# Block rows loaded in 256-byte pieces from ScalarE's queue and transposed by VectorE, in a routed feed-forward kernel

## What is computed

```
x = x + attention(layernorm(x), ctx)          # 16 heads of 16
x = x + ffn(layernorm(x))
ffn: logits = xf @ Wr + br;  top 2 of 8 experts, softmax over the two
     h = xf @ W1[e] + b1[e]                   # 256 -> 1024, halves a and g
     out_e = (silu(a) * g) @ W2[e] + b2[e]    # 512 -> 256
     out = sum over the two chosen experts of gate * out_e
```

## Time and profile before

| | |
|---|---|
| median of three runs | 1309.9 us |
| profiled execution, its own time | 1309.45 us |
| its span | 1307.6 us |
| mean granted TensorE clock | 0.959 of full |
| PE, DVE, ACT, POOL busy, share of the span | 91%, 77%, 57%, 48% |

### The profile page before, as it was taken

The page is one execution under the profiler, slowest core; times in us unless marked ns, Lnnn a source line. Parts: engine busy times, 40 slices in busy tenths (PEclk is TensorE's granted clock), DMA queues, the critical chain, the costliest instruction groups (busy, mean ns, idle before and its releaser), DMA issues.

```text
span 1307.6 us, 38188 instructions
## 1 busy us (share of the span) xinstructions
PE 1189.3 (91%) x12680; PEld 1047.7 (80%) x12681; DVE 1001.4 (77%) x2933; ACT 750.2 (57%) x1497; POOL 625.2 (48%) x729
## 2 busy tenths in 40 slices
PE   5999999999999999730699999999999999999986
PEld 4677777777777777520599999999999999999986
DVE  5788888888888878735487888888788888877764
ACT  5676666666666665412456555555655556565452
POOL 5346666666666665542043444444344443432334
PEclk9999999999999999755699999999999999999998
DMA  5123332333333322217667676676767776676553
GB/s 172 35 87 93 98 96 93 100 98 98 101 98 102 94 69 74 76 61 234 192 172 176 170 186 161 182 165 178 179 164 188 162 182 167 175 181 155 147 149 37
DMA packets 106958, 174.78 MB, mean 134 GB/s; under 512 B 13600, under 2 KB 82400, under 8 KB 106848
## 3 DMA queue, kind: packets, MB, share of 16 engines
q1 hardware_dynamic: 77808, 134.45, 32.1%
q0 software_dynamic: 26592, 36.46, 16.7%
q10 hardware_dynamic: 2448, 2.44, 0.6%
HBM read 125.17 MB, written 47.60 MB: 132 GB/s over the span
## 4 chain that ended last, share of the span: by engine, by line
PE 41%; DMA 8%; issue 2%; POOL 1%; SPq 1%; DVE 0%; ACTq 0%; ACT 0%; POOLq 0%; DVEq 0%
PE bank L1071 9%; PE bank L1072 8%; PE bank L1073 8%; DMA out_rows<-y_gated,block_tokens 6%; PE bank L1086 4%; PE bank L1087 4%; PE bank L1088 4%; PE bank L1060 2%; DMA w_raw<-in_L_ffn_W 1%; PE bank L1089 1%; POOL out_rows L1319 1%; SPq L1020 0%; DMA routed_rows<-block_rows 0%; DVE act L1274 0%; ACTq L994 0%
## 5 line engine op out<-in xcount | busy, mean ns | idle before, releaser
L1319 POOL DMA_INDIRECT out_rows<-y_gated,block_tokens x142 | 267.2, 1882 | 435.0 <-DVE y_gated L1289 339.0
L1071 PE MATMUL bank<-block_T_hi,w_hi 128*128 128x256 f32 x1136 | 330.8, 291 | 10.1 <-DVE block_T_lo L1264 10.1
L1073 PE MATMUL bank<-block_T_hi,w_lo 128*128 128x256 f32 x1136 | 319.0, 281 | 0.0
L1072 PE MATMUL bank<-block_T_lo,w_hi 128*128 128x256 f32 x1136 | 319.0, 281 | 0.0
L1071 PEld LDWEIGHTS bank<-block_T_hi,w_hi 128*128 128x128 f32 x1136 | 216.2, 190 | 11.8 <-DVE block_T_lo L1264 8.0
L1072 PEld LDWEIGHTS bank<-block_T_lo,w_hi 128*128 128x128 f32 x1136 | 216.0, 190 | 0.0
L1073 PEld LDWEIGHTS bank<-block_T_hi,w_lo 128*128 128x128 f32 x1136 | 215.3, 190 | 0.0
L1157 ACT ACTIVATE act_hi<-act 128x512 fp32r<-128x512 f32 x142 | 89.8, 632 | 195.3 <-DVE act L1274 195.3
L491 ACT ACTIVATE probs_T<-bank 128x512 f32<-128x512 f32 x256 | 132.2, 603 | 98.3 <-PE bank L322 98.3
L1247 DVE TENSOR_TENSOR w_lo<-w_raw,w_hi 128x1024 fp32r<-128x1024 f32 x142 | 167.7, 1222 | 11.3 <-ACT w_hi L1134 10.9
L599 DVE TENSOR_REDUCE row_max<-bank 128x4 f32<-128x512 f32 x256 | 158.9, 683 | 22.3 <-PE bank L303 22.3
(11 more groups left out here) (159 smaller groups left out, 2494.6 us busy)
## 6 DMA issues: line engine op xcount, KB each, us to landing
w_raw<-in_L_ffn_W SPq DMA_DIRECT2D x71, 1024.0 KB
block_rows<-routed_rows SPq DMA_DIRECT2D x71, 272.0 KB
x_in<-in_x SPq DMA_DIRECT2D x64, 128.0 KB, 2.5
ctx_T<-in_ctx SPq DMA_DIRECT2D x16, 512.0 KB, 4.2
x_res<-in_x SPq DMA_DIRECT2D x64, 128.0 KB, 2.5
out_rows<-x SPq DMA_DIRECT2D x64, 128.0 KB, 2.3
w_raw<-in_L_ffn_W SPq DMA_DIRECT2D x8, 512.0 KB, 7.9
out_rows<-y_gated,block_tokens POOLq DMA_INDIRECT x142, 4.3
```

Source lines behind the costliest of these rows:

```text
L1071: mm(dst, w1h[:, k, c, at:at + P], xh[:, k, c, :], start=(c == 0), stop=False)
L1072: mm(dst, w1h[:, k, c, at:at + P], xl[:, k, c, :], start=False, stop=False)
L1073: last = mm(dst, w1l[:, k, c, at:at + P], xh[:, k, c, :], start=False, stop=(c == KC - 1))
L1319: nc.gpsimd.indirect_dma_start(out=out[:, :], out_offset=bass.IndirectOffsetOnAxis(ap=tk[:, u % U, t:t + 1], axis=0), in_=yg[:, u % 2, t, ...
```

## The change

Only `experts` changes.

- SP no longer loads block rows. Its slot holds `load_w1` alone, which is now two DMAs of 512 KB instead of one of 1 MB; the rows of W1 go to other partitions, matching the new order of the features.
- ScalarE's queue loads block rows, at the end of its slot, for block b+3. There are five DMAs for a block: four that fill 32 partitions each with pieces of 256 bytes (1024 pieces in all), and one for the last 16 floats of each row (256 pieces of 64 bytes) into a buffer of its own, `block_marks`. The two waits of `load_rows` come along. At the start the first two loads stand ahead of `w1_hi(0, 0)`, and the third behind `x_hi(0, 0)`.
- The four transposes on PE are gone. VectorE transposes all 32x32 squares of 128x512 in one instruction (`square`), between `w1_lo` and `mult` of the first half, from SBUF to SBUF.
- `x_hi` and `x_lo` read SBUF instead of PSUM. The moving operand of the 48 up matmuls is read in eight runs of 32 elements instead of one of 256. The idle rows have a buffer of their own.

```diff
-        xb = sb("block_rows", [P, 2, ET, ROW], F32)
+        xb = sb("block_rows", [P, 2, NJ, KC, DT], F32)
+        xm = sb("block_marks", [P, 2, ET, ROW - D], F32)
+        xT = sb("block_T", [P, NJ, KC, DT], F32)
+        pad_t = sb("idle_rows", [P, ET, ROW], F32)
...
         @block.sync
-            def load_rows(i, u):
...
-                sp.dma_start(w1r[:, u % 2], ... "(c p) n -> p c n" ...).then_inc(s_w1[u % 2], 16)
+                w = w1....rearrange("(p c i) n -> c p i n", c=KC, i=DT)
+                for c in range(KC):
+                    sp.dma_start(w1r[:, u % 2, c, :], w[c]).then_inc(s_w1[u % 2], 16)
...
             def slot(i, u):
                 if real(i, u + 2):
-                    load_rows(i, u + 2)
                     load_w1(i, u + 2)
...
         @block.tensor
-            def to_T(i, u):   # four transposes, L1053 to L1062
...
-                        mm(dst, w1h[:, k, c, at:at + P], xh[:, k, c, :], start=(c == 0), stop=False)
+                        mm(dst, w1h[:, k, c, at:at + P], xh[:, k, :, c, :], start=(c == 0), stop=False)
...
         @block.scalar
+                act.wait_ge(s_pd, 16 * (E + 2))
+                load_rows(0, 0)
+                load_rows(0, 1)
                 w1_hi(0, 0)
                 x_hi(0, 0)
+                load_rows(0, 2)
+
+            def load_rows(i, u):
+
+                r = act.value_load(tab[0:1, 1, bass.ds(blk(i, u), 1)], min_val=0, max_val=E * REG)
+                if real(i, u - 2):
+                    act.wait_ge(s_xT, n(i, u - 2))
+                    act.wait_ge(s_meta, n(i, u - 2))
+                rows = xs[bass.ds(r, EB), :]
+                for p in range(NP):
+                    act.dma_start(xb[p * DT:(p + 1) * DT, u % 2].rearrange("k j c i -> k j (c i)"),
+                                  rows[:, p * KC * DT:(p + 1) * KC * DT].rearrange("(j k) m -> k j m", k=DT)
+                                  ).then_inc(s_ld[u % 2], 16)
+                act.dma_start(xm[:, u % 2], rows[:, D:ROW].rearrange("(t p) c -> p t c", p=P)).then_inc(s_ld[u % 2], 16)
...
                 act_hi(i, u, 1)
+                if real(i, u + 3):
+                    load_rows(i, u + 3)
...
         @block.vector
+            def square(i, u):
+
+                dve.wait_ge(s_ld[u % 2], n2(i, u, NP + 1))
+                if real(i, u - 1):
+                    dve.wait_ge(s_xl, n(i, u - 1))
+                V.transpose(xT[:].rearrange("p j c k -> p (j c k)"),
+                            xb[:, u % 2].rearrange("p j c i -> p (j c i)")).then_inc(s_xT, 1)
...
             def slot(i, u):
                 if real(i, u + 1):
                     w1_lo(i, u + 1)
+                    square(i, u + 1)
                 mult(i, u, 0)
```

More of the change, by code:

```diff
@@ L912, in experts @@
     HM = FC // 2
+    NJ = EB // DT
+    NP = P // DT
     with ExitStack() as ctx:
@@ L938, in experts @@
         prf = sb("idle_at_f", [1, E], F32)
-        xb = sb("block_rows", [P, 2, ET, ROW], F32)
+        xb = sb("block_rows", [P, 2, NJ, KC, DT], F32)
+        xm = sb("block_marks", [P, 2, ET, ROW - D], F32)
+        xT = sb("block_T", [P, NJ, KC, DT], F32)
+        pad_t = sb("idle_rows", [P, ET, ROW], F32)
         tk = sb("block_tokens", [P, U, ET], I32)
         gt = sb("block_gates", [P, U, ET], F32)
-        pad = xb[:, 1]
-        xh = sb("block_T_hi", [P, 2, KC, EB], F32R)
-        xl = sb("block_T_lo", [P, 2, KC, EB], F32R)
+        pad = pad_t[:]
+        xh = sb("block_T_hi", [P, 2, NJ, KC, DT], F32R)
+        xl = sb("block_T_lo", [P, 2, NJ, KC, DT], F32R)
         sa = sb("silu_a", [P, FC, EB], F32)
@@ L985, in n, with n2 @@
             return i * (U * per) + (u * per + (per if done is None else done))
-        def n2(i, u):
-            return i * (U // 2 * 16) + (u // 2 + 1) * 16
+        def n2(i, u, parts):
+            return i * (U // 2 * 16 * parts) + (u // 2 + 1) * 16 * parts
         def idle_rows(eng, experts):
@@ L1012, in load_w1 @@
                     sp.wait_ge(s_w1l, n(i, u - 2, KC))
-                sp.dma_start(w1r[:, u % 2], w1.rearrange("e k n -> (e k) n")[bass.ds(e * D, D), :]
-                             .rearrange("(c p) n -> p c n", p=P)).then_inc(s_w1[u % 2], 16)
+                w = w1.rearrange("e k n -> (e k) n")[bass.ds(e * D, D), :].rearrange("(p c i) n -> c p i n", c=KC, i=DT)
+                for c in range(KC):
+                    sp.dma_start(w1r[:, u % 2, c, :], w[c]).then_inc(s_w1[u % 2], 16)
             def first():
@@ L1025, in first @@
                 load_w1(0, 0)
-                sp.wait_ge(s_pd, 16 * (E + 2))
-                load_rows(0, 0)
-                load_rows(0, 1)
                 load_w1(0, 1)
@@ L1050, in first @@
                 nc.tensor.transpose(bank[5][:, 0:E * 2 * FC], b1r[:], ident[0:E * 2 * FC, 0:E * 2 * FC]).then_inc(s_b1t, 1)
-                to_T(0, 0)
-            def to_T(i, u):
[L1055 to L1062, removed]
             def up(i, u, bk, half, side):
@@ L1068, in up @@
                     at = side * F + (HM * half + m) * P
-                    dst = bk[:, m * EB:(m + 1) * EB]
+                    dst = bk[:, m * EB:(m + 1) * EB].rearrange("p (j k) -> p j k", k=DT)
                     for c in range(KC):
-                        mm(dst, w1h[:, k, c, at:at + P], xh[:, k, c, :], start=(c == 0), stop=False)
-                        mm(dst, w1h[:, k, c, at:at + P], xl[:, k, c, :], start=False, stop=False)
-                        last = mm(dst, w1l[:, k, c, at:at + P], xh[:, k, c, :], start=False, stop=(c == KC - 1))
+                        mm(dst, w1h[:, k, c, at:at + P], xh[:, k, :, c, :], start=(c == 0), stop=False)
+                        mm(dst, w1h[:, k, c, at:at + P], xl[:, k, :, c, :], start=False, stop=False)
+                        last = mm(dst, w1l[:, k, c, at:at + P], xh[:, k, :, c, :], start=False, stop=(c == KC - 1))
                 return last
@@ L1103, in slot @@
                     up(i, u, bank[2 * half + 1], half, 1).then_inc(s_g, 1)
-                    if half == 0 and real(i, u + 1):
-                        to_T(i, u + 1)
                 if real(i, u - 1):
@@ L1125, in first @@
                 act.dma_start(xs[E * REG:E * REG + EB, :].rearrange("(t p) c -> p t c", p=P), pad).then_inc(s_pd, 16)
+                act.wait_ge(s_pd, 16 * (E + 2))
+                load_rows(0, 0)
+                load_rows(0, 1)
                 w1_hi(0, 0)
                 x_hi(0, 0)
+                load_rows(0, 2)
[10 more added lines that the diff above has]
+                act.dma_start(xm[:, u % 2], rows[:, D:ROW].rearrange("(t p) c -> p t c", p=P)).then_inc(s_ld[u % 2], 16)
             def w1_hi(i, u):
-                act.wait_ge(s_w1[u % 2], n2(i, u))
+                act.wait_ge(s_w1[u % 2], n2(i, u, KC))
                 if real(i, u - 2):
@@ L1139, in x_hi @@
                     act.wait_ge(s_g, n(i, u - 2, 2))
-                nc.scalar.activation(xh[:, u % 2].rearrange("p c n -> p (c n)"), bank[4][:, :], ACT.Copy).then_inc(s_xh, 1)
+                nc.scalar.activation(xh[:, u % 2].rearrange("p j c k -> p (j c k)"),
+                                     xT[:].rearrange("p j c k -> p (j c k)"), ACT.Copy).then_inc(s_xh, 1)
             def silu(i, u, half):
@@ L1240, in first @@
                 dve.wait_ge(s_b1, 1)
+                square(0, 0)
                 meta(0, 0)
```

11 lines of the change are left out of this document (6 added, 5 removed).

## The result

The changed kernel takes 1647.9 us (median of four runs, 1643.6 to 1651.0) against 1310.5 us on the same chip: ratio 1.258, interval 1.255 to 1.261. It is slower, as forecast, but by 337 us where I had forecast 112, and outside my range of 1358 to 1485.

The account below looks back on a forecast made before the run. It took PE as the bound, 9.14 us a block, and the ScalarE-VectorE round afterwards: 7.05 + 0.70 - 0.54 + 3.65 = 10.86 us. With PE's second block at 649.6, 68 rounds and the ending gave 1422 us, range 1358 to 1485.

Parts of the forecast that it names:

- W1 in two DMAs costs SP one more issue: SP's weight load in the expert stage: one more issue, no cost, since weights have a whole block of lead.
- The DMA engines: Expert stage: 1280 new pieces at 15 ns, 1.2 us over 16 engines, 4.8 at most; a bound only at the far end.
- The round through ScalarE and VectorE: Each expert block: grows from 7.05 to 10.86 us, with 3.65 us in ScalarE's queue, and becomes the bound.
- the cover of 2.09 us: Expert block before the change: spare time of the 7.05 us ScalarE-VectorE round within PE's 9.14 us block.
- verdict B: Theory from the experiments: ScalarE's queue stalls by itself on 1280 small pieces a block, whatever W1 does.
- `square`: VectorE's transpose between `w_lo` and `mult`: taken as 0.70 us, bounds 0.43 and 0.86; adds 0.70 to the round.
- PE's block: PE in the expert stage: without the transposes' 0.35 us, 8.79 instead of 9.14 us a block.
- The clock: PE's clock in the expert stage: the expected gap of 2.07 us a block lies at the harmless one of 2.01.
- The start: Start of the expert stage: PE's second block begins at 649.6 instead of 643.89, 5.7 us lost once.
- The rivals: Issues hide, PE stays bound 4%; effects cancel 2%; adds become the bound 12%; strided operand slows matmuls 4%.
- The adds: Rival in the expert stage: POOL's adds become the bound, period 11.55 us, 1469 us in all; chance 12%.
- twice their spacing: Rival on PE: strided operand slows up matmuls to 0.238 us, block 14.5 us, 1670 us in all; chance 4%.

Follow-up runs that it names:

- e2: The kernel before, with only W1's load in the changed form (two DMAs of 4 x 32 rows): 1548.8 us, ratio 1.181.
- e1: The changed kernel, with W1 loaded as four DMAs of 32 partitions over all engines: 1441.95 us, ratio 1.0995.
- e10: The changed kernel with W1 in one DMA of 1 MB, block rows still from ScalarE's queue: ratio 1.0719.
- e5: e1 with the row loads behind the first `silu` instead of at the slot's end, for block u+2 instead of u+3: ratio 0.9958.
- e6: The kernel before, with its one DMA of block rows moved to the end of ScalarE's slot: ratio 0.9946.
- e3: The changed kernel with block rows from SP's queue and W1 in four DMAs over all engines: 1295.0 us, ratio 0.9878.
- e4: The changed kernel with block rows issued from SP's queue, W1 still in its two DMAs on four engines: 1592.85 us, ratio 1.2143.
- e7: e3 with W1 in one DMA of 1 MB instead of four: ratio 0.9838.
- e8: e7 with the operand of the 48 up matmuls in one contiguous run: ratio 0.980; run once more, 1259.56 us, ratio 0.9809.
- e9: e2 with W1's two DMAs as 8 x 16 rows instead of 4 x 32: ratio 1.0144 against the kernel before.
- e11: e2 with the one DMA of block rows moved to the end of ScalarE's slot: ratio 1.2403 against the kernel before.

## Why the prediction was wrong

- **The step that failed** is "W1 in two DMAs costs SP one more issue; SP has nothing else to do, and the weights have a whole block of lead". It was costed at nothing. I counted issues and the lead, and took the transfer's own rate as unchanged, without looking at how the two DMAs' dimensions lie. In the runs that step alone is worth 238 us on the kernel before (e2) and 206 us of the 337 on the changed one (e1). The lead of a block doesn't help when the transfer itself lasts longer than PE's block of 9.14 us: one W1 takes 12.7 us from its first packet to its last (e2), 4.4 in the kernel before, because four of the 16 DMA engines carry it and not all.
- **The DMA engines** were costed as one resource of 16 (1.2 to 4.8 us over 16). The price of a piece was right, 17 ns against 15. But the share of a page is a mean over 16 engines: 0.47 looked free when four of them were full (W1 alone 84% of four engines' time).
- **The round through ScalarE and VectorE** was right. Forecast 10.86 us, of them 3.65 in the queue; measured 10.46 and 3.39 (e10), 10.96 and 3.92 (e1). e1, the kernel I had in mind, took 1442 us, where I had said 1422; as a ratio 1422 us are 1.086, between e10's 1.072 and e1's 1.0995. e5 shows that the cost comes from the place in the queue. Of the cover of 2.09 us, e6 shows 0.8 to be there and e3 the 0.70 of `square`; the whole was not tried. That the kernel got slower, as forecast, was not luck, since this cost alone does it. But most of the measured time isn't explained by it: W1 alone costs 282 us (e4).
- **The issue that stalls** I had not thought of at all: an engine's queue waits when its DMAs aren't taken. It made ScalarE's queue 22% of the chain, and invites the wrong verdict B. That moving an issue to another queue is worth nothing held for one DMA (e6, within 1%), and not for five at the end of the slot (e10, 7%).
- **`square`**: 0.70 us, as taken. **PE's block**: 8.96 us (e3) instead of 8.79, 0.08 of the difference from the strided operand (e7 to e8).
- **The clock**: I judged a gap of 2.07 us harmless, from a single one of 2.01 us. It isn't always: in e1 the gaps are 1.5 to 2.9 us, and after the one of 2.27 us at 1009 the matmuls start 0.21 us apart from 1010.7 on, the 1.2 GHz level; the mean clock of 700 to 1200 us is 0.96. With gaps of 1.1 to 1.7 us (e10) it stayed at 1.00, with those of 6 to 9 us in the changed kernel it was 0.83. In none of them did it decide the time, since ScalarE and VectorE hardly waited for PE.
- **The start**: I had `w_hi(0, 1)` at 641.8 us; it was at 654.4, and at 645.5 in e1. The first row load was issued at 640.9 instead of e1's 632.6, so the idle rows it waits for landed later beside W1 on four engines.
- **The rivals**: none was W1. The adds did not become the bound in the changed kernel (no part of the chain), though they hold up the last blocks of the kernel before and of e9. The matmuls did not slow down to twice their spacing.

## What to carry to other kernels

When a DMA's order is changed, look at the outermost dimension of both its sides before anything else, and compare its share in a stretch where it alone is waited for with 4/16, 8/16 and 16/16; a count of its packets in flight says it outright. Issues of DMAs on an engine's queue cost what no wait covers: find the place in the slot where this engine waits for another, and put them there, or use a queue that has nothing else. Check the lead too: a load moved to the end of another engine's slot may be issued much later than before (e11). A change that looks bad as a whole can hold a good part; here the kernel with the squares on VectorE was 1.9% faster once the two loads around them were mended, 1.3% of it from PE's shorter block.

## What the runs showed of the hardware that I had not expected

- Two DMAs of 4 x 32 strided rows of 4 KB: four packets in flight, 12.7 us for 1 MB (e2) and 14.0 beside 1280 small pieces (the changed kernel); of 8 x 16 rows: eight in flight, 7.1 us, and 1.4% on the whole kernel.
- An issue of 256 pieces on ScalarE's queue took 0.35 us when accepted and up to 7.8 us when not, with 1280 pieces a block beside four crowded engines; with 256 a block it was never longer than 0.39 (e11). From SP's queue the same DMAs took up to 3.6 us (e4).
- The same 1 MB in four DMAs of 32 partitions (e3) kept the DMA engines busy for 0.90 of the time, in one DMA of 128 partitions (e7) for 0.75: its packets of 4 KB took 293 ns in the mean in e3 and 191 in e7.
